# A fused feed-forward, attention, feed-forward kernel on Trainium2: the seam between the first two stages, with the casts of batch 0's stacks moved from ScalarE to VectorE

## The reference

```
x = x + 0.5 * ffn(layernorm(x))
x = x + attention(layernorm(x))      # itself: y = layernorm(x); y + gate * out(y)
x = x + 0.5 * ffn(layernorm(x))

ffn(x):        h = silu(x Wg^T) * (x Wu^T);  return h Wd^T          # 128 -> 384 -> 128, integer weights
attention(y):  h = rmsnorm(y); q, k, v = h Wq, h Wk, h Wv           # 4 heads, 2 key/value heads, 32 wide
               q, k = q/|q|, k/|k|
               out = softmax(causal(q k^T) * exp(t)) v;  return y + gate * out Wo
```

## Time and profile before

| | us |
|---|---|
| median of 3 runs | 463.25 |
| lowest, highest | 463.16, 465.41 |
| the profiled execution | 463.7 |
| its span on the core | 461.9 |

### The profile page before, as it was taken

How to read it: one execution, slowest core, us unless ns; L and a number is a source line. 1 busy time by engine, 2 the same in 40 slices (tenths; PEclk the granted TensorE clock), 3 DMA queues, 4 the chain that set the end, 5 groups by cost and what they waited for, 6 DMA issues and landing times.

```text
span 461.9 us, 10471 instructions
## 1 busy us (share of the span) xinstructions
PE 414.1 (90%) x3747; PEld 214.0 (46%) x3747; DVE 357.9 (77%) x872; ACT 383.5 (83%) x546; POOL 260.6 (56%) x321
## 2 busy tenths in 40 slices
PE   0779988988998999999999999999999998999994
PEld 0346655663434435435435435335334334767654
DVE  5889998799499869869779779687556937878654
ACT  4799988875886988988988988988977998999960
POOL 5499987983625535435444444441141465999950
PEclk9999999999999999999999999999999999999999
DMA  5586521516109054065062072082070022547462
GB/s 159 130 158 148 70 46 36 103 25 125 36 4 173 10 94 91 1 112 73 0 123 58 0 135 47 1 132 53 1 138 0 16 34 47 136 92 138 92 115 73
DMA packets 119150, 34.94 MB, mean 76 GB/s; under 512 B 101568, under 2 KB 119104, under 8 KB 119104
## 3 DMA queue, kind: packets, MB, share of 16 engines
q1 hardware_dynamic: 117824, 34.02, 38.7%
q10 hardware_dynamic: 1280, 0.33, 0.3%
HBM read 4.98 MB, written 4.19 MB: 20 GB/s over the span
## 4 chain that ended last, share of the span: by engine, by line
PE 55%; DVE 15%; issue 12%; ACT 7%; POOL 7%; DMA 2%; DVEq 1%; SPq 0%; POOLq 0%; ACTq 0%
PE ps L507 13%; PE ps L706 11%; PE ps L687 9%; PE ps L711 9%; DVE H L327 4%; PE ps L569 4%; PE ps L558 4%; ACT PT L817 3%; PE ps L594 2%; DVE X L1021 2%; DVE AN L1008 2%; PE ps L691 2%; POOL OL L281 2%; POOL RF L925 1%; DVE bns L306 1%
## 5 line engine op out<-in xcount | busy, mean ns | idle before, releaser
L817 ACT ACTIVATE PT<-ps,k_exp 128x1024 f32<-128x1024 f32 (+1 forms) x192 | 162.1, 900 | 20.0 <-PE ps L691 14.7
L507 PE MATMUL ps<-XT,WT 128*128 128x512 f16 x384 | 95.3, 387 | 10.6 <-ACT SG L476 4.7
L687 PE MATMUL ps<-QKT 128*128 128x512 f16 (+3 forms) x384 | 87.1, 328 | 11.4 <-ACT PT L817 9.3
L706 PE MATMUL ps<-PT,V 128*32 128x512 f32 (+3 forms) x768 | 81.8, 498 | 0.0
L711 PE MATMUL ps<-PT,ones 128*32 128x512 f32 (+3 forms) x768 | 79.6, 486 | 0.0
L433 POOL TENSOR_TENSOR HL<-H,HH 128x1024 f16<-128x1024 f32 x31 | 67.2, 2167 | 10.1 <-ACT HH L482 7.9
L327 DVE SCALAR_TENSOR_TENSOR H<-SG,k_isilu,ps 128x1536 f32<-128x1536 f32 x32 | 57.8, 1807 | 14.1 <-PE ps L507 5.4
L281 POOL TENSOR_TENSOR OL<-ON,OH 128x512 f16<-128x512 f32 x15 | 18.2, 1216 | 77.3 <-ACT OH L277 77.3
L507 PEld LDWEIGHTS ps<-XT,WT 128*128 128x128 f16 x384 | 34.5, 99 | 56.2 <-issue 17.4
L687 PEld LDWEIGHTS ps<-QKT 128*128 128x128 f16 x384 | 27.8, 97 | 69.3 <-ACT PT L817 60.1
L458 ACT ACTIVATE XN<-X,NB,RS 128x128 f32<-128x128 f32 x128 | 52.4, 482 | 2.3 <-POOL NB L405 2.3
(11 more groups left out here) (139 smaller groups left out, 649.1 us busy)
## 6 DMA issues: line engine op xcount, KB each, us to landing
result<-X SPq DMA_DIRECT2D x15, 256.0 KB, 2.5
X<-in_L_attn_x SPq DMA_DIRECT2D x7, 512.0 KB, 4.5
X<-in_L_attn_x SPq DMA_DIRECT2D x2, 256.0 KB, 4.8
XT<-w_int SPq DMA_TRANSPOSE x32, 3.1
AXT<-AS SPq DMA_TRANSPOSE x16, 2.8
QKT<-ST SPq DMA_TRANSPOSE x16, 5.6
w_int<-in_L_ffn_w_gate SPq DMA_DIRECT2D x1, 192.0 KB, 4.0
w_int<-in_L_ffn_w_up SPq DMA_DIRECT2D x1, 192.0 KB, 4.3
```

The source lines that it names most:

```text
L507: i = e.matmul(out[:, j, :], WT[:, wp, w * NJ + j, :], XT[k % 2][:, xp, :], start=a == 0, stop=a == len(passes) - 1)
L687: i_ = e.matmul(o, QKT[k % 2][:, i // TPC, NH + hp, i % TPC * P:(i % TPC + 1) * P], QKT[k % 2][:, qc, 2 * hp + h, CH - n:CH], start=True, ...
L706: e.matmul(PVD[HD * h:HD * h + HD, 0, CH - n:CH], V[k % 2][:, i, v0:v0 + HD], PT[g % 2][:, h, 0:n], start=i == 0, stop=done, skip_group_ch ...
L817: e.activation(PT[g % 2][:, 2 * hp:2 * hp + 2, 0:n], SCORES[hp][:, :, 0:n], ACT.Exp, scale=k_exp[:, 0:1]).then_inc(a_exp, 1)
```

## The change

Three edits, all at the seam.

**1. VectorE casts the stacks of batch 0.** `first_stack_hi` on VectorE takes the place of ScalarE's L849 for chunks 0 and 1, right behind QN, with the two float16 copies right behind the cast. For chunk 0 that is ahead of the last H; for chunk 1 the normalisation of chunk 2 now stands behind the cast and the copies.

**2. GpSimdE takes the low parts of chunk 0's stack ahead of HL(14),** no longer behind it, and chunk 13's residual is taken out of the row ahead of the last H on VectorE and put behind it.

**3. GpSimdE casts x of chunks 2 and 3** (`first_x_hi`), no longer ScalarE.

The core of the diff:

```diff
-            early += [(hidden, 0)]
+            early += [(hidden, 0)] + [(residual, NC - 3)] * (1 - ph)
...
-            x_hi(2, 0)
             exps(0, 0, 0)
...
-                        if k == 0 and g == 1:
-                            x_hi(3, 1)
...
             stack_lo(1, 1)
-            x_lo(2, 0)
-            x_lo(3, 1)
+            for m in range(2, 4):
+                first_x_hi(m, m - 2)
+                x_lo(m, m - 2)
...
+            def first_stack_hi(m):
+
+                e.wait_ge(a_qn, m + 1)
+                e.tensor_copy(ST[m][:, :, :, 0, :].rearrange("p h t d -> p t h d"), QN[m][:, :, :, :])\
+                    .then_inc(a_hi, 1)
...
                 unit(0, 20, 1, 1)
+                first_stack_hi(1)
+                stack_hi2(1, 1)
                 normalise(2, 2, 2)
-                stack_hi2(1, 1)
...
-                                  11: first(("rstds_a", 2)), 14: first(("stack_lo", 0)),
+                                  11: first(("rstds_a", 2)),
                                   15: first(("rstds_b", 3))},
-                     {13: first(("rstds_b", 2), ("rstds_a", 3))})
+                     {13: first(("rstds_b", 2), ("rstds_a", 3)), 14: first(("stack_lo", 0))})
...
-                                 15: first(("stack_hi", 0), ("v_out", 1, 1), ("squares", 1))})
+                                 15: first(("v_out", 1, 1), ("squares", 1))})
             e.activation(warm[:, :], lt_t[:, :], ACT.Exp)
-            att_act(e, False, ("stack_hi", 1))
...
-                     13: stage("sums"), 14: stage("unit"), 15: stage("stack")})
+                     13: stage("sums"), 14: stage("unit"),
+                     15: lambda: ffn_dve(e, 0, [("residual", NC - 3)])})
```

More of the change, by code:

```diff
@@ L379, in ffn_dve @@
             if only is not None:
-                ops = dict(stats=stats, aggregate=aggregate, moments=moments, hidden=hidden, x_lo=x_lo)
+                ops = dict(stats=stats, aggregate=aggregate, moments=moments, hidden=hidden, x_lo=x_lo, residual=residual)
                 for name, c in only:
@@ L930, in first_x_hi @@
                 e.wait_ge(a_xn, m + 1)
+                if m >= 2:
+                    e.wait_ge(d_x[half], 16)
                 e.tensor_copy(AS[half][:, 0, :, :], AN[half][:, :, :]).then_inc(a_xh0, 1)
             def x_lo(m, half):
-                if isinstance(m, int) and m < 2:
+                if isinstance(m, int) and m < 4:
                     e.wait_ge(a_xh0, m + 1)
                 else:
-                    e.wait_ge(a_xh, m - 1)
+                    e.wait_ge(a_xh, m - 3)
                 e.tensor_tensor(AS[half][:, 1, :, :], AN[half][:, :, :], AS[half][:, 0, :, :],
@@ L1123, in att_dve @@
                 unit(0, 10, 0, 0)
-                return
-            if first == "stack":
+                first_stack_hi(0)
                 stack_hi2(0, 0)
```

## The result

The changed kernel takes 468.36 us, the median of 6 runs (465.94 to 470.15). The kernel before, run beside it on the same chip, takes 463.31 (6 runs, 463.16 to 465.43). The ratio is 1.0085, with a 95% interval of 1.0055 to 1.0114. The prediction of 463.8 (462.5 to 465.8) was wrong: the change makes the kernel slower, by 5.05 us between the medians and by 3.9 by the ratio (2.5 to 5.3). The profiled execution took 468.5 us, its span is 466.7.

The account below looks back on a forecast made before the run. The prediction took the seam as bound by ScalarE's first two exponentials, then TensorE. Down products delayed the first scores by 1.50 us, freed ScalarE casts left the first exponential 0.52 later: 463.25 + 0.52 = 463.8 us, range 462.5 to 465.8.

Parts of the forecast that it names:

- TensorE falls to its slower clock in the gap: Rival, chance 0.10: after the pause before down(14), matmuls run at half pace, 465.5 to 469.1 us, taken as 467.5.
- The sum: Main forecast of the seam, chance 0.50: first exponential 0.52 us later, carried to the end, median 463.8 us.
- The cast at 0.56: Chunk 0's stack cast on VectorE behind QN(0): 0.56 us for 768 elements, bounds 0.42 and 1.18.
- one free copy and one held for 1.18: Chunk 0's two stack copies on VectorE: the second held beside GpSimdE, so the last H starts 0.82 us later.
- the last H, down(14) and QKT(0)'s issue: At the seam: predicted at QN(0) + 2.90, + 5.51 and + 3.57 us.
- residual(13)'s place as the cause of the pause: Before down(14): it waits for residual(13), now behind the last H, leaving TensorE idle 2.88 us.
- the first scores: Behind the fillers on TensorE: predicted at 108.48 us instead of 106.98, 1.50 later.
- the second scores of group 1: On TensorE, waiting for the second exponential: predicted at QN(0) + 14.82 us, against 14.30 before.
- free copies: Rival, chance 0.13: chunk 0's copies aren't held, the last H starts at 98.66, first exponential 0.30 us sooner, 463.0 us.
- exponentials alone: Rival, chance 0.09: down products don't decide, the first exponential comes 1.0 us or slightly more sooner, 462.2 us.
- A second term: At group 4: QKT(1), issued at 111.8, lands 5.48 us later at 117.3, hidden with 0.2 us to spare.
- nothing before it is touched: Upstream of the seam: everything before QN(0), at 96.58 to 97.54 us, was taken as unchanged.

Follow-up runs that it names:

- experiment 3: The changed kernel with chunk 13's residual put back ahead of the last H; 466.65 us, ratio 1.0058 to the kernel before.
- experiment 4: The kernel before with only chunk 1's stack cast on VectorE and x of chunks 2 and 3 cast on GpSimdE; 464.14 us, ratio 0.9993.
- experiment 1: The changed kernel with twelve matmuls nobody reads filling TensorE's pause ahead of down(14); 467.25 us, ratio 1.0065 to the kernel before.
- experiment 8: The kernel before with the query/key/value weights' cast moved from VectorE to ScalarE; 460.96 us, ratio 0.9929.
- experiment 9: The changed kernel with the query/key/value weights' cast moved from VectorE to ScalarE; 464.12 us, ratio 0.9993 to the kernel before.
- experiment 2: The kernel before with only chunk 13's residual moved behind the last H; 467.16 us, ratio 1.0063.
- experiment 5: The changed kernel with twelve fill matmuls in the pause and 64 never-run matmuls ahead of TensorE's program; 467.24 us, ratio 1.0066 to the kernel before.
- experiment 6: The changed kernel with chunk 13's residual ahead of the last H and 64 never-run matmuls ahead of TensorE's program; 464.98 us, ratio 1.0027.
- experiment 7: The kernel before with one extra GpSimdE operation ahead of chunk 1's low parts, so QKT(1) is issued late; 466.23 us, ratio 1.0024.

## Why the prediction was wrong

**The step that failed** is the weighing of the rival "TensorE falls to its slower clock in the gap". The sum named the pause, 2.88 us, and it measured 2.85; the rival named the mechanism, the place and the price, "the time is 465.5 to 469.1; I take 467.5". The sum let down(14), down(15) and the fillers run at full pace behind that pause: 1.95 us, 1.79 to the start of the fillers, and 1.73 from there to the first scores. They took 2.89, 3.55 and 1.93, which is 2.9 us more and lies in the rival's 1.7 to 5.3. Its 467.5 is near the measured 468.36 in part by luck, since some 1.5 us of that time stand upstream. What was wrong was the chance of 0.10. The prediction had one pause to compare, 1.77 us, shorter than the new one by 1.1, and no row at all of a longer pause with full pace behind it. A pause longer than any in the running kernel should have had at least an even chance of being the deciding thing. The granted clock of 1.00 in the earlier trace rows is no evidence either: the trace of the kernel before has no record of the clock ahead of 20.6 us, and the view shows 1.00 where there is none. The pace there, 2.72 us for what took 1.47 later, is the lower one. The Trainium skill, "TensorE: Matmul & The Clock Gate", Part 1, had said that idleness takes the clock down; the runs agree (0.50 behind 2.85 us of idleness). The prediction cited it and then gave it too little weight.

**What held.** The cast at 0.56, midway between two sizes; one free copy and one held for 1.18, as in the earlier trace rows, and 1.35 us from the cast's end to the last H (the sum added 1.35, though it had worked out 1.37 from the rows); the last H, down(14) and QKT(0)'s issue within 0.02 us; residual(13)'s place as the cause of the pause; with the clock held by fills, the first scores within 0.16 and the second scores of group 1 within 0.16 (14.98 against 14.82). The "free copies" rival is out (1.18). The "exponentials alone" rival is right in direction for the parts that don't touch the residual, and its 1.0 us is nearly there: experiment 3 has 0.49 at group 1, experiment 4 has 0.92 at group 4.

**A second term would have failed too,** if the clock had not hidden it. The prediction has "it lands 5.48 later at 117.3" and "Group 4 wants it at 117.02 + 0.52 = 117.54". The issue was right to 0.01 us in experiment 1, but the landing took 7.4. The price was taken from QKT(0), whose flight meets no code load, and the 0.2 us to spare hid that. The slower landings, 7.3 and 7.5, stood in the trace of the kernel before at 170 and 303 us; with them "with 0.2 us to spare" would have read 1.5 to 1.7 us late. In the changed kernel TensorE was so late that QKT(1) landed in time (issued 114.17, landed in 5.7, group 4 at 121.98). So of the 2.75 us that the fills gave back only 1.1 reached the end: 3.6 us of loss at the seam became 2.5.

**The measured difference is larger than the seam's.** Of 5.16 us between the two kernels in profiles, 1.53 stand upstream, in unchanged code. The medians on a common base of experiments 8 and 9 give 3.2. The prediction took the time of one profiled execution as fixed up to QN(0) ("nothing before it is touched"); that is right for the code and wrong for the time. Whether the change itself tilts that race is open. The profiles of the changed kernel and of experiments 1, 2, 3 and 5 have QN(0) at 97.9 to 98.8, those of the kernel before and of experiments 4, 6 and 7 at 96.5 to 96.6. The weights' cast took 2.2 us in each of the first five and 1.2 in each of the others, and there are edits at the seam in both kinds.

## What to carry to other kernels

Before moving a step behind another, look at the longest pause that TensorE will have, and compare it with those behind which the traces show full pace. Here falls came behind pauses from 1.95 us on, and full pace behind pauses up to 1.96, so a pause near or beyond the longest seen with full pace needs its own term at half the clock and a good chance, and filling it with idle matmuls tests it in one run. Take the landing of a transfer from the slowest of its kind in the whole trace and not from one or the median where the margin is tenths of a microsecond, and look for what else comes onto the DMA engines in its flight. And where VectorE and GpSimdE start within 0.1 us of each other, the order of the two can change from kernel to kernel and be worth up to 2 us, as here: move one of them to another engine before fine work on anything behind it.

## What the runs showed of the hardware

- Pauses of TensorE and the granted clock behind them, in the profiles: at the seam 1.12, 1.54, 1.56 and 1.60 us, with 1.00 all through; 1.95, 2.07, 2.07, 2.85 and 2.88 us, a fall to 0.50, which came within 1.5 us of the restart and lasted 6.8 us at down(14) and 3.4 us at group 4. At about 25 us in the kernel 1.77, 1.88 and 1.96 us had full pace behind them. So there was no fall behind 1.96 and one behind 1.95; the runs don't say what counts besides the length.
- VectorE's casts, copies and tensor_scalar operations beside GpSimdE aren't slowed in proportion but end 0.1 to 0.2 us behind the end of a GpSimdE operation, as if held by it: 0.28 became 1.18, 1.20 became 2.19, and two operations of 0.60 together became 1.44 or 3.40.
- A transpose into QKT, 5.6 us as a rule, took 7.0 to 7.9 in 36 of 208 cases, and each of these had a 16 KB load of the instruction queue 5.0 to 5.9 us behind its issue; eleven others with a load 4.95 to 5.6 us behind the issue took 5.5 or 5.6. Which starts it isn't shown.
